# SyncE saves the query's upper part to DRAM before the two lower parts are ready

## What is computed

```python
x = x + L0_xattn(layernorm(x), ctx); x = x + L0_ffn(layernorm(x))   # 8 heads of 64; 8 experts, top 2
x = x + L1_xattn(layernorm(x), ctx); x = x + L1_ffn(layernorm(x))   # 16 heads of 8; 4-bit fake quantization
x = x + L2_xattn(layernorm(x), ctx); x = x + L2_ffn(layernorm(x))   # 16 heads of 8, mask; 8-bit fake quantization
x = x + L3_xattn(layernorm(x), ctx); x = x + L3_ffn(layernorm(x))   # 8 heads of 16, 1 + tanh; ternary weights
```

## Time and profile before

| | |
|---|---|
| median of three runs | 861.32 us |
| the profiled execution's own time | 858.38 us |
| its span, first to last instruction | 856.6 us |
| TensorE busy | 581.3 us (68%) |
| VectorE busy | 536.8 us (63%) |
| ScalarE busy | 399.4 us (47%) |
| GpSimd busy | 255.4 us (30%) |
| mean granted TensorE clock | 0.794 of full speed |

### The profile page before, as it was taken

How to read it: one execution, slowest core, us unless ns; L and a number is a source line. 1 busy time by engine, 2 the same in 40 slices (tenths; PEclk the granted TensorE clock), 3 DMA queues, 4 the chain that set the end, 5 groups by cost and what they waited for, 6 DMA issues and landing times.

```text
span 856.6 us, 19147 instructions
## 1 busy us (share of the span) xinstructions
PE 581.3 (68%) x5772; PEld 400.5 (47%) x5772; DVE 536.8 (63%) x1653; ACT 399.4 (47%) x893; POOL 255.4 (30%) x515
## 2 busy tenths in 40 slices
PE   4599999987788857878513322699998027875342
PEld 3478787875444444545201101366665015653121
DVE  2477676752677746777688885366675663335673
ACT  1355555561222216666427654555554014445674
POOL 2111111101455533332124226333331113333420
PEclk9989999995999958899655555599999556995555
DMA  8422222220000023334000001133331013550001
GB/s 241 118 63 63 62 61 61 61 56 10 1 0 0 0 56 84 94 101 102 11 0 0 0 0 26 40 87 87 92 88 29 0 29 94 145 142 26 0 2 49
DMA packets 103973, 46.73 MB, mean 55 GB/s; under 512 B 84144, under 2 KB 93424, under 8 KB 103920
## 3 DMA queue, kind: packets, MB, share of 16 engines
q1 hardware_dynamic: 103920, 46.09, 21.5%
HBM read 26.13 MB, written 19.92 MB: 54 GB/s over the span
## 4 chain that ended last, share of the span: by engine, by line
PE 31%; issue 24%; DVE 17%; POOL 9%; DVEq 6%; ACT 5%; DMA 3%; POOLq 3%; SPq 1%; ACTq 0%
PE bank L482 3%; POOL small L1304 2%; PE bank L512 2%; PE bank L423 2%; PE bank L465 2%; PE bank L417 2%; DVE mx L1559 2%; PE bank L434 2%; DVE small L1391 1%; DMA scratch_q<-q_parts 1%; PE bank L586 1%; PE bank L440 1%; PE bank L558 1%; DMA stacks<-scratch_q 1%; POOL stats L1184 1%
## 5 line engine op out<-in xcount | busy, mean ns | idle before, releaser
L1559 DVE TENSOR_REDUCE mx<-bank 128x4 f32<-128x512 f32 x160 | 104.0, 684 | 24.5 <-PE bank L423 22.7
L874 ACT ACTIVATE probs<-bank 128x512 f32<-128x512 f32 x160 | 90.9, 595 | 55.1 <-PE bank L444 50.0
L1184 POOL TENSOR_TENSOR stats<-stats,half_neg 128x1 f32<-128x1 f32 x48 | 26.4, 550 | 186.2 <-DVE stats L1530 178.8
L482 PE MATMUL bank<-probs,v_slot 128*9 128x128 f32 x1024 | 44.5, 288 | 3.4 <-ACT probs L874 0.9
L1574 DVE SCALAR_TENSOR_TENSOR resid<-bank,w_bias_cols,q_parts 128x128 f32<-128x128 f32 x48 | 16.8, 350 | 47.6 <-ACT q_parts L920 47.6
L1541 DVE TENSOR_TENSOR x_sb<-bank,x_sb 128x128 f32 (+1 forms) x64 | 18.5, 289 | 43.5 <-PE bank L586 23.3
L1235 POOL CAST q_parts<-resid 128x128 bf16<-128x128 f32 x48 | 14.2, 296 | 99.2 <-DVE resid L1574 99.2
L906 ACT ACTIVATE xn_t<-bank 128x128 f32<-128x128 f32 x64 | 17.7, 277 | 54.6 <-PE bank L507 52.8
L507 PE MATMUL bank<-w_ident,xn 128*128 128x128 f32 x64 | 21.6, 338 | 31.5 <-DVE xn L1535 20.5
L440 PE MATMUL bank<-stacks 48*128 48x128 bf16 x512 | 39.2, 227 | 2.4 <-DVE shift_t L1595 1.6
L444 PE MATMUL bank<-shift_t,pick_bf 64*128 64x128 bf16 x512 | 39.0, 226 | 0.0
(11 more groups left out here) (297 smaller groups left out, 1729.1 us busy)
## 6 DMA issues: line engine op xcount, KB each, us to landing
stacks<-scratch_k SPq DMA_DIRECT2D x64, 96.0 KB, 2.2
stacks<-scratch_q SPq DMA_DIRECT2D x64, 96.0 KB, 2.2
scratch_k<-k_parts SPq DMA_DIRECT2D x48, 96.0 KB, 1.8
scratch_q<-q_parts SPq DMA_DIRECT2D x48, 96.0 KB, 1.9
scratch_k<-k_parts SPq DMA_DIRECT2D x48, 64.0 KB, 1.7
scratch_q<-q_parts SPq DMA_DIRECT2D x48, 64.0 KB, 1.8
stacks<-scratch_k SPq DMA_DIRECT2D x16, 192.0 KB, 2.6
stacks<-scratch_q SPq DMA_DIRECT2D x16, 192.0 KB, 2.5
```

The lines of the kernel that those rows point to most:

```text
L482: last = mm(bank[4][32 * j:32 * j + w, cols], v, probs[:, (s * U + u) % 4, j * T:(j + 1) * T], start=layer < 3, stop=True, skip_group_chec ...
L874: activation(probs[:, slot, :], bank[2 + u % 2][:, :], ACT.Tanh if layer == 3 else ACT.Exp, scale=float(d) ** -0.5).then_inc(sm["p"], 1)
L1184: tt(stats[:, s, 9:10], stats[:, s, 8:9], half_neg[:, :], ALU.pow).then_inc(ln_rstd, 1)
L1559: reduce(mx[:, sM, at * UNIT:(at + 1) * UNIT], bank[u % 2][:, :].rearrange("p (h k) -> p h k", h=UNIT), AX.X, ALU.max).then_inc(sm["mx"], 1)
```

## The change

The wait for GpSimd's signal moves from before the three writes to between the first and the second; in its old place stands a wait for ScalarE's signal. The writes, their order, sizes and semaphore are as before.

```diff
                     wait(sp, sm["st"], (t - SLOTS + 1) * (H // UNIT))
                     stack_up(k_stack, s, scratch_k[layer - 1, t])
-                    sp.wait_ge(sm["parts"], t + 1)
+                    sp.wait_ge(sm["q_h"], t + 1)
                     row = 0
                     for part, n in TERMS:
+                        if part == 1:
+                            sp.wait_ge(sm["parts"], t + 1)
                         sp.dma_start(scratch_q[s, row:row + n].rearrange("j r k -> r j k"),
                                      q_parts[:, s, part:part + 1, :].to_broadcast([P, n, T])
                                      ).then_inc(q_saved[s], 16)
```

## The result

The changed kernel takes 853.36 us (median of 22 runs, 850.36 to 857.97), the kernel before 858.16 us in as many runs (852.31 to 863.76). The ratio is 0.9947, with a 95% interval of 0.9929 to 0.9965: 4.5 us less (3.0 to 6.1). The direction and the class (within 1%) are as forecast; the size is 2.5 times the forecast 1.8 us, and the time lies 1.0 us under the range. Part of that last miss is the starting point: the median of three runs from which the forecast started, 861.32, stands 3.2 us over the median of 22.

The account below looks back on a forecast made before the run. Many short stages in turn were taken to bound the kernel. Terms of −1.76 us in layer 1 and −0.44 and +0.4 in layer 3 summed to −1.8, from the 861.32 us median to 859.5 us; range 854.4 to 863.8 us.

Parts of the forecast that it names:

- In layer 2: Layer 2's query trip through DRAM: TensorE's work covers it, so the early write gains nothing, 0 us.
- the price of a step in layer 1: SyncE's writes in layer 1: one issue less behind GpSimd's signal, 0.44 us taken rather than 0.53, landing unchanged.
- met waits in layer 3: Layer 3, SyncE's 11 late steps: one more already met wait each, at 0.035 us, costs 0.4 us.
- four crossings: Layer 1, steps 4, 9, 13 and 15, where the chain passes the writes' landing: 0.44 us each, 1.76 us gained.
- step 4 of layer 3: The one step of layer 3 where the chain passes the writes' landing: the first write goes ahead, gaining 0.44 us.
- Layer 3 nets to nothing: Layer 3 as a whole: −0.44 us at step 4 against +0.4 us for already met waits in 11 late steps.
- Refilled: Layer norm's way through GpSimd, or the maxima, ends next and gives most gain back: about 861.0 us, chance 0.22.
- Not acting: SyncE comes late everywhere, as in layer 3, with both signals already there: no gain, 861.3 us, chance 0.04.
- The held write: The first two writes held the last one's landing; an early first write saves 3.7 us more: 855.8, chance 0.06.
- SyncE's stream longer: Layer 3, steps 5 to 15: the added wait costs up to 0.48 us a step, 864.4 us, chance 0.08.
- The clock: Layers 1 and 3: shorter TensorE waits avoid all five half-clock stretches, 8.5 us more, 851.0 us, chance 0.05.
- The range: Whole kernel's time after the change: 854.4 to 863.8 us, upper end at the highest earlier run, chance 0.92.

Follow-up runs that it names:

- the lengthened: Two more 32 KB writes between GpSimd's signal and the three writes, in layer 2 alone, against the kernel before: ratio 1.0006, +0.5 us.
- doubly shortened trip: Upper part written on ScalarE's signal and middle part on its own signal, in layer 2 alone, against the kernel before: ratio 1.0007, +0.6 us.
- the repeat: The unaltered change profiled and timed once more, against the kernel before: 853.64 us, ratio 0.9958, −3.6 us.
- The three runs in layer 1: Layer 1 alone, against the kernel before: early first write, −2.4 us; middle part also on its own signal, −5.4 us; two more 32 KB writes, +6.2 us.
- layer 3 alone: The early first write in layer 3 only, layers 1 and 2 as before, against the kernel before: ratio 0.9986, −1.2 us.
- a larger edit: In layer 3 only, upper and middle parts written on their own signals and key's reads behind the writes, against the kernel before: ratio 0.9957, −3.7 us.
- the best version: The change plus middle part's write on its own signal in all layers and layer 3's key reads behind the writes, against the kernel before: 850.19 us, ratio 0.9911.

## Why the prediction was right or wrong

*Direction, class and mechanism: right.* One issue leaves the path behind GpSimd's signal; the landing stays; nothing that was moved meets anything. In layer 2 nothing comes of it: forecast 0, and nothing clear of 0 by the lengthened and by the doubly shortened trip.

*What failed is the sum.* Two of its terms were wrong, and the traces show both: the price of a step in layer 1, 0.44 us where 0.55 was measured, and the 0.4 us for met waits in layer 3, which cost nothing. With these two put right, the prediction's own four crossings and step 4 of layer 3 give 5 × 0.55 = 2.75 us. The rest up to 4.5 is not shown to belong to any one term.

*Layer 1: right term, too small.* The forecast was 4 × 0.44 = 1.76 us. Two things were off, both on the low side. The price: of 0.44 and 0.53 I took the lower, arguing that the second write would keep its issue of 0.48; it takes 0.39 after a pause, and with 0.02 in the landing the step gains 0.55. The count: the chain of one execution showed four crossings, while the unchanged layer 1 in the experiments' profiles shows four to six (with the change, five in the profile after and three in the repeat). The three runs in layer 1 give 2.4 / 0.55 = 4.4, 5.4 / 1.11 = 4.9 (its landing measured in the same edit in all layers) and, lengthened, 6.7, with intervals of 1.5 to 7.3, 3.0 to 6.8 and 4.3 to 8.8. Five crossings fit all three, four only the first two, so that the count was too low is likely and not shown. Five at 0.55 are 2.75, inside the measured 0.8 to 4.0.

*Layer 3: a term that should have been nothing.* "Layer 3 nets to nothing" was −0.44 + 0.4, and the 0.4 was a price for eleven met waits. They cost nothing: 0.05 us from issue to issue with the wait and without. Without that term the forecast stands at −2.2. That SyncE's stream is late in most steps and sets the end is borne out by the +7.5 us for two more issues. But I read from it that eleven steps could never gain. SyncE's lateness is not fixed: over steps 5 to 15 the last write started on average 2.6 us behind GpSimd's end in the profile before, 1.6 in the profile after and 2.6 again in the repeat; with layer 3 alone 1.1, in the other profiles with layer 3 unchanged 1.7 to 2.8. If a saving of an early step brings SyncE back on time, the first write can go ahead again; that this happened is not shown. In the run with layer 3 alone SyncE waited for GpSimd at line 362 in 7 steps of 16:

```profile
SPq L362 <- POOL q_parts L1240: 6.0, 7, 1.4
```

In the earlier trace rows it did so in 5, but with layer 3 unchanged it was 5 or 6 in other profiles, and in both profiles of the whole change 5. How much of the change's gain lies in layer 3 stays open: −1.2 us with an interval from −3.3 to +1.0. That layer 3 has something to give is shown by the −3.7 us only for a larger edit.

*What is left.* With the prices as measured, five crossings in layer 1 give 2.75 and step 4 of layer 3 gives 0.55, 3.3 us together; the change's two intervals, 3.0 to 6.1 and 1.7 to 5.6, both hold that. Between it and the 4.5 stand scatter, whatever layer 3 gives beyond step 4, and the clock.

*The rivals.* Refilled: no, in layer 1 the gain came through. Not acting: no, by the timeline. The held write: no. Two landings after the change, with the first write issued 1.3 and 1.0 us ahead of the last, in the chain of layer 1:

```profile
326.65 3.82 DMA scratch_q<-q_parts
...
333.58 3.67 DMA scratch_q<-q_parts
```

SyncE's stream longer: no, by the gap of 0.05.

*The clock: not in the way that was forecast, but not excluded.* The short stretches at half clock in layers 1 and 3 did not go away, by the windows. Yet the time of an execution does go with its granted clock. Among the runs of the kernel before beside the experiments (four sets of 23 to 29), 0.01 more clock went with 2.6 to 3.9 us less. Their mean clock is 0.794 to 0.796, that of the 22 runs of the change 0.800: worth some 1 to 2.5 us of the 4.5, by an estimate from these figures. In the repeat the clocks are equal (0.796 both), and there the gain is 3.6 us. Whether the change itself raises the clock stays open: the two kernels with a lengthened trip in layers 1 and 3 ran at 0.791 and 0.788, but the same kernel of the change ran at 0.800 once and at 0.796 once.

*The range.* It was built on the three runs shown; their median was high by 3.2 us. That the forecast is compared with a kernel before that is itself a sample belonged into the low end as well as into the high one.

## What to carry to other kernels

Where a chain of dependent writes waits for the last of several inputs, let each write go on its own input's signal: what was saved here is the issue of each write that goes ahead, times the steps that the chain really crosses, while the landing of the last stayed nearly as it was. One execution's chain gives that count only roughly when two loops are nearly equally long, so make the suspected step longer by a known amount, one stage at a time, and divide. Look also at the granted clock of every run before calling the last microsecond a gain of the change. And look for what a serially issuing engine does before a wait that it could do during it: the key's reads behind the writes are a candidate, part of the best version, though moving them was not shown to gain by itself.

## What was not expected of the hardware

- A DMA issue on SyncE's queue mostly took 0.31 to 0.39 us after a pause and 0.42 to 0.54 right behind another (a few took up to 1.9); a met wait between two of them added nothing to the 0.05 us from one to the next.
- In the chains of layer 1, away from the first steps, a 32 KB write mostly landed 1.45 us after its issue when the writes ahead of it had gone out earlier, 1.56 to 1.64 with one to four issued just ahead of it.
- The same code ahead of layer 1 took 301.3 to 306.4 us in the sixteen profiles, with 24 to 37 us of it at half clock.
- Around the first steps of the loop the last write's landing took 3 to 3.8 us in layers 1 and 3, before and after the change (3.21 and 3.66 in the earlier trace rows, 3.82 and 3.67 above). What delays it was not tried.
